# A graph kernel's first stage in groups of four blocks, with every fourth PSUM bank copied by VectorE

## What is computed

```python
e = concat(u, i)            # u = p_u * (diag_u[:, None] * x_u @ W_u) + x_u ; i likewise with W_i
h = adj @ (adj.T @ e)
out = (h - mu) * rsqrt(var + eps) * gamma + beta + x
x = layernorm(x + out)
```

## Time and profile before

| | us |
|---|---|
| median of 3 runs | 1492.0 |
| lowest and highest | 1490.86, 1493.19 |
| the profiled execution | 1491.23 |
| its span in the trace | 1489.4 |
| TensorE busy in the span | 1472.9 |
| VectorE busy | 612.3 |
| ScalarE busy | 257.8 |
| DMA queue of SyncE, share of 16 engines' span | 90.4% |

### The profile page before, as it was taken

The page is one execution under the profiler, slowest core; times in us unless marked ns, Lnnn a source line. Parts: engine busy times, 40 slices in busy tenths (PEclk is TensorE's granted clock), DMA queues, the critical chain, the costliest instruction groups (busy, mean ns, idle before and its releaser), DMA issues.

```text
span 1489.4 us, 17202 instructions
## 1 busy us (share of the span) xinstructions
PE 1472.9 (99%) x6462; PEld 683.0 (46%) x6462; DVE 612.3 (41%) x1281; ACT 257.8 (17%) x535; POOL 61.3 (4%) x66
## 2 busy tenths in 40 slices
PE   8999999999999999999999999999999999999997
PEld 6555555555555543334444344444444444444332
DVE  5755565655555568424332553324111021110432
ACT  3333334343434320000100000100000000000110
POOL 0000000000000002100000011010000000000010
PEclk9999999999999999999999999999999999999999
DMA  9999999999999998999988588876498869988997
GB/s 318 371 413 416 417 417 415 386 414 407 383 417 398 394 390 321 422 421 420 335 318 306 212 366 314 308 271 229 149 334 307 294 228 359 336 321 306 373 420 284
DMA packets 121537, 517.87 MB, mean 348 GB/s; under 512 B 20300, under 2 KB 20340, under 8 KB 71540
## 3 DMA queue, kind: packets, MB, share of 16 engines
q1 hardware_dynamic: 119568, 516.46, 90.4%
q10 hardware_dynamic: 1892, 0.35, 0.1%
HBM read 410.61 MB, written 106.17 MB: 347 GB/s over the span
## 4 chain that ended last, share of the span: by engine, by line
issue 99%; POOLq 0%; POOL 0%; DVE 0%
POOL power_out L539 0%; POOLq L537 0%; POOLq L539 0%; DVE rows L1024 0%; POOL ident L532 0%; POOLq L534 0%; POOL ident L534 0%; POOLq L1284 0%
## 5 line engine op out<-in xcount | busy, mean ns | idle before, releaser
L839 PE MATMUL ps_u<-blk,vectors 128*128 128x512 f32 (+1 forms) x1904 | 682.7, 594 | 1.3 <-DMA blk<-a_transposed 0.7
L839 PEld LDWEIGHTS ps_u<-blk,vectors 128*128 128x128 f32 (+1 forms) x1904 | 273.5, 170 | 369.8 <-issue 366.6
L578 ACT ACTIVATE blk<-ps_turn 128x512 f32<-128x512 f32 x400 | 202.2, 625 | 330.0 <-PE ps_turn L664 328.7
L1198 DVE TENSOR_TENSOR part<-part,ps_u 64x512 f32<-64x512 f32 (+1 forms) x40 | 27.4, 685 | 356.2 <-PE ps_u L839 355.8
L705 PE MATMUL ps_h<-blk,u_rows 128*64 128x512 f32 x720 | 164.4, 598 | 0.0
L940 DVE TENSOR_REDUCE row_part<-blk 128x4 f32<-128x2048 f32 x68 | 152.4, 2278 | 0.1
L924 DVE TENSOR_TENSOR part<-part,ps_h 128x512 f32<-128x512 f32 x80 | 55.0, 687 | 184.4 <-PE ps_h L705 184.4
L664 PE MATMUL ps_turn<-ident,blk 128*128 128x128 f32 x1072 | 126.0, 276 | 3.0 <-DMA blk<-in_adj 3.0
L664 PEld LDWEIGHTS ps_turn<-ident,blk 128*128 128x128 f32 x1072 | 117.8, 142 | 23.1 <-issue 19.5
L688 PE MATMUL ps_u<-blk,e 128*64 128x512 f32 x544 | 123.8, 594 | 0.0
L539 POOL TENSOR_TENSOR power_out<-power_in,minus_half 128x4 f32<-128x4 f32 x60 | 60.6, 1010 | 1424.4 <-DVEq L987 1424.4
(11 more groups left out here) (123 smaller groups left out, 625.2 us busy)
## 6 DMA issues: line engine op xcount, KB each, us to landing
blk<-a_transposed SPq DMA_DIRECT2D x276, 1024.0 KB, 6.6
a_transposed<-blk SPq DMA_DIRECT2D x100, 1024.0 KB, 14.2
blk<-in_adj SPq DMA_DIRECT2D x67, 1024.0 KB, 12.3
nat_far<-in_adj SPq DMA_DIRECT2D x32, 1024.0 KB, 12.8
early_blk<-a_transposed SPq DMA_DIRECT2D x12, 1024.0 KB, 8.0
nat_far<-a_transposed SPq DMA_DIRECT2D x2, 1024.0 KB, 11.3
rows<-in_x SPq DMA_DIRECT2D x10, 128.0 KB, 9.2
out<-rows SPq DMA_DIRECT2D x10, 128.0 KB, 3.5
```

The costliest lines, as they stand in the source:

```text
L578: nc.scalar.activation(blk[:, n % RING, t, :], ps_t[t][:, :], ACT.Copy)\
L839: mm = pe.matmul(acc, left, tiles[:, t, :], start=first, stop=last)
L1198: V.tensor_tensor(part[parts, cols], part[parts, cols], ps_both[r % 2][parts, :], ALU.add)\
```

## The change

The first column is put in another order. Rows of x are loaded ahead of their block, blocks 0 to 2 come in quarters, and the first e product stands in the middle of block 1's turn. The product x W is two matmuls with a block-diagonal W of 128 x 128 instead of four of 64 x 64, and has a place of its own in each of the two ps_h banks. The factors for users and for items have a semaphore each.

From block 10 on there are groups of four blocks (the last has two): four e products, then four h products, then four turns. `u_rows` becomes two tiles in turn (`u_columns`). From block 11 on ScalarE copies three banks of a block and VectorE the fourth (`evacuate_last_bank`), behind the four adds of the group.

Three smaller edits: two of the last h products move beside other blocks (`SOON_H`), the second last add moves ahead of a wait for a root (`soon`), and `add_y` waits for the last block of its own group of sums.

```diff
-    SOON_BEGUN, SOON_H = 3, 7
+    SOON_BEGUN, SOON_H = 3, {(1, 1): 7, (2, 2): 8}
...
+    IN_QUARTERS, GROUP = 3, 4
...
-                sp.wait_ge(at_evacuated, TB * (n + 1))
+                sp.wait_ge(at_evacuated, act_evacuated(n))
+                if n > NB:
+                    sp.wait_ge(last_bank_evacuated, n - NB)
...
-                if n == 0:
-                    for c in range(TB - 1):
-                        sp.dma_start(nat(0)[:, c, :], a_blocks[:, c, 0:BLK]).then_inc(quarter_loaded[c], 16)
-                    sp.dma_start(nat(0)[:, TB - 1, :], a_blocks[:, TB - 1, 0:BLK]).then_inc(nat_loaded[0], 16)
+                if n < NB:
+                    tiles = slice(n * TB, (n + 1) * TB)
+                    sp.dma_start(rows[:, tiles, :], x_rows[:, tiles, :]).then_inc(x_loaded[n], 16)
+                if n < IN_QUARTERS:
+                    for c in range(TB):
+                        sp.dma_start(nat(n)[:, c, :], a_blocks[:, n * TB + c, 0:BLK])\
+                            .then_inc(quarter_loaded[n][c] if c < TB - 1 else nat_loaded[n], 16)
                 else:
                     sp.dma_start(nat(n), a_blocks[:, i * TB:(i + 1) * TB, j * BLK:(j + 1) * BLK])\
                         .then_inc(nat_loaded[n % NAT], 16)
-                if n < NB:
-                    tiles = slice(n * TB, (n + 1) * TB)
-                    sp.dma_start(rows[:, tiles, :], x_rows[:, tiles, :]).then_inc(x_loaded[n], 16)
                 for k in range(n_behind(n - 1), n_behind(n)):
                     store(k)
...
-                for t in range(TB):
+                for t in range(TB if n <= NB else TB - 1):
                     act.wait_ge(turned, TB * n + t + 1)
                     nc.scalar.activation(blk[:, n % RING, t, :], ps_t[t][:, :], ACT.Copy)\
                         .then_inc(at_evacuated, 1)
...
-                if i > 0:
-                    pe.wait_ge(xw_used, i)
+                if i == 0:
+                    pe.wait_ge(w0_cleared, 1)
                 pe.wait_ge(w_i_loaded if i >= UB else consts_loaded, 32 if i >= UB else 16 * N_CONSTS)
-                for t in range(TB):
-                    xw_t = (xw_even if t % 2 == 0 else xw_odd[i % 2])[:, t // 2, :]
-                    mm = pe.matmul(xw_t, x_in_turned[i % 2][half(t), t // 2 * P:(t // 2 + 1) * P],
-                                   w0[half(t), int(i >= UB), :], start=True, stop=True)
+                for u in range(HT):
+                    mm = pe.matmul(xw_in[i % 2][:, u * P:(u + 1) * P], x_in_turned[i % 2][:, u * P:(u + 1) * P],
+                                   w0[:, int(i >= UB)].rearrange("p k f -> p (k f)"), start=True, stop=True)
                 mm.then_inc(xw_ready, 1)
...
+            def turn_quarters(n, between={}):
 
                 for c in range(TB):
                     if c < TB - 1:
-                        pe.wait_ge(quarter_loaded[c], 16)
+                        pe.wait_ge(quarter_loaded[n][c], 16)
                     else:
-                        pe.wait_ge(nat_loaded[0], 16)
+                        pe.wait_ge(nat_loaded[n], 16)
                     for t in range(TB):
-                        mm = pe.transpose(ps_t[t][:, c * P:(c + 1) * P], nat(0)[:, c, t * P:(t + 1) * P], ident[:, :])
+                        if c == 0 and n > 0:
+                            pe.wait_ge(at_evacuated, TB * (n - 1) + t + 1)
+                        mm = pe.transpose(ps_t[t][:, c * P:(c + 1) * P], nat(n)[:, c, t * P:(t + 1) * P], ident[:, :])
                         if c == TB - 1:
                             mm.then_inc(turned, 1)
+                    if c in between:
+                        between[c]()
...
             def h_part(n):
                 pe.wait_ge(u_ready, n // NB + 1)
-                pe.wait_ge(at_evacuated, TB * (n + 1))
+                pe.wait_ge(at_evacuated, act_evacuated(n))
+                if n > NB:
+                    pe.wait_ge(last_bank_evacuated, n - NB)
...
-            turn_first()
+            def first_e():
+                turn_diag()
+                times_w(0)
+
+            def first_u():
+                u_part(0)
+                times_w(1)
+
             turn_x_in(0)
-            turn_diag()
-            times_w(0)
-            for n in range(NB):
-                turn_block(n + 1)
+            turn_quarters(0, {1: first_e})
+            turn_x_in(1)
+            turn_quarters(1, {1: first_u})
+            for n in range(1, NB):
                 if n + 1 < NB:
                     turn_x_in(n + 1)
                 u_part(n)
                 if n + 1 < NB:
                     times_w(n + 1)
-            for p in range(COLUMN, BLOCKS // 2):
-                u_part(2 * p)
-                u_part(2 * p + 1)
-                if p % COLUMN == 0:
-                    u_turn_back(p // COLUMN - 1)
-                if p > COLUMN:
-                    turn_block(2 * p)
-                turn_block(2 * p + 1)
-                if p == BLOCKS // 2 - 1:
+                if n + 1 < IN_QUARTERS:
+                    turn_quarters(n + 1)
+                else:
+                    turn_block(n + 1)
+            def turn_group(four):
+                for n in four:
+                    if n > NB:
+                        turn_block(n)
+
+            for four in groups:
+                last = four[-1] == BLOCKS - 1
+                for n in four:
+                    u_part(n)
+                if last:
+                    turn_group(four)
                     u_turn_back(NB - 1)
-                h_part(2 * p - NB)
-                h_part(2 * p + 1 - NB)
+                for n in four:
+                    if n % NB == 0 and (n == NB or n != four[0]):
+                        u_turn_back(n // NB - 1)
+                for n in four:
+                    h_part(n - NB)
+                if not last:
+                    turn_group(four)
+                    if four[-1] % NB == NB - 1:
+                        u_turn_back(four[-1] // NB)
...
-                    if k != SOON_H:
+                    if k not in SOON_H.values():
                         last_h_part(k)
                 for b in row_0[e - 1] if 1 <= e <= NB - 2 else ():
-                    if blocks[b][1:3] == (1, 1):
-                        last_h_part(SOON_H)
+                    if blocks[b][1:3] in SOON_H:
+                        last_h_part(SOON_H[blocks[b][1:3]])
                     multiply_block(b)
...
-                diag_i = diag[:, tiles].rearrange("p (t k) -> p k t", k=2)
-                for k in range(2):
-                    V.tensor_tensor(by_pairs(ta)[:, k], (xw_even, xw_odd[i % 2])[k],
-                                    diag_i[:, k].unsqueeze(2).broadcast_to([P, HT, F]), ALU.mult)
+                V.tensor_tensor(ta[:, :, :], xw_in[i % 2].rearrange("p (t f) -> p t f", t=TB),
+                                diag[:, tiles].unsqueeze(2).broadcast_to([P, TB, F]), ALU.mult)
...
-                V.reduce_sum((u_rows if j < NB - 1 else u_last)[:, :, :], back_halves[j % 2], AX.X).then_inc(u_ready, 1)
+                V.reduce_sum(u_columns[j % 2][:, :, :], back_halves[j % 2], AX.X).then_inc(u_ready, 1)
...
             copy_x_in(0)
-            dve.wait_ge(par_loaded, 32)
-            V.tensor_tensor(par_prod[:, :], par[:, :, 0], par[:, :, 1], ALU.mult)
-            dve.drain()
-            dve.wait_ge(diag_turned, 1)
-            V.tensor_scalar(diag[:, 0:UT], diag_in[:, 0:UT], par_prod[:, 0:1], None, ALU.mult)
-            V.tensor_scalar(diag[:, UT:NT], diag_in[:, UT:NT], par_prod[:, 1:2], None, ALU.mult)
-            dve.drain()
+            dve.wait_ge(par_u_loaded, 16)
+            weigh_diag(0, slice(0, UT))
             make_e(0)
-            for c in range(TB - 1):
-                dve.wait_ge(quarter_loaded[c], 16)
             for n in range(NB):
                 if n + 1 < NB:
                     copy_x_in(n + 1)
+                for c in range(TB - 1 if n < IN_QUARTERS else 0):
+                    dve.wait_ge(quarter_loaded[n][c], 16)
                 sum_rows(n)
+                if n == 1:
+                    dve.wait_ge(par_i_loaded, 16)
+                    weigh_diag(1, slice(UT, NT))
                 if n + 1 < NB:
                     make_e(n + 1)
             copy_u(0)
-            for p in range(COLUMN, BLOCKS // 2):
-                sum_rows(2 * p)
-                sum_rows(2 * p + 1)
-                if p % COLUMN == 0:
-                    copy_u_rows(p // COLUMN - 1)
-                if p % COLUMN == COLUMN - 1:
-                    copy_u(p // COLUMN)
-                if p == BLOCKS // 2 - 1:
+            def evacuate_last_bank(n):
+                dve.wait_ge(turned, TB * (n + 1))
+                dve.wait_ge(at_stored[n % RING], 16 * (n // RING))
+                V.tensor_copy(blk[:, n % RING, TB - 1, :], ps_t[TB - 1][:, :]).then_inc(last_bank_evacuated, 1)
+
+            for four in groups:
+                last = four[-1] == BLOCKS - 1
+                for n in four:
+                    sum_rows(n)
```

(67 more changed lines are left out.)

13 lines of the change are left out of this document (11 added, 2 removed).

## The result

The changed kernel takes **1566.1 us**, the kernel before 1492.6 in the same runs: a ratio of 1.0487, 95% interval [1.0465, 1.0509]. It was forecast slower, by 8.8 us; it is slower by 73.6.

The account below looks back on a forecast made before the run. TensorE, busy 1472.9 of 1489.4 us, was taken as the bound. The terms summed to +8.8 on the profiled 1491.2, giving 1500.0, or 1500.8 us for the median; range 1488 to 1509.

Parts of the forecast that it names:

- Term d: Groups of four: loads 0.6 early, but 2.0 late at blocks 40, 60 and 80; +6.0 us, bounds 0 and 10.
- Term a: First stage: fewer changes between kinds of TensorE work, 0.32 a round saved 22 times; -7.0 us.
- Term b: First group, blocks 10 to 13: TensorE waits 0.9 and 3.5 on VectorE; +4.4 us, bounds 3.5 to 4.6.
- Term c: ScalarE's constant loads behind blocks 11 and 15 delay evictions, waits about 1.2 and 3.8; +5.0 us, from 0 to 5.3.
- Term e: Between two groups: VectorE's chain of copy, sums and add comes late in some groups; +4.8 us, bounds 2.5 and 13.
- Term f: Five groups: turning back u between the two products instead of beside turns adds two changes of kind; +1.6 us.
- Term g: First column: earlier first product and shorter rounds, less 1.3 for the lower clock; -3.6 us, bounds -5.5 and -1.5.
- Term h: The ends: a turn in the first layer's end no longer waits, -1.0; an add in the last sweep, -1.4 us.
- transfers have room: Rival: DMA queue not full, issues take 0.33, loads land in time; sum -2.3, 1489.7 us; chance 0.24.
- transfers are the bound: Rival: at 2.7 a transfer, a group's eight need 21.6, so every group waits 0.6; 1506 us; chance 0.10.
- VectorE is the bound: Rival: VectorE's chain between groups is 0.45 longer and 22 groups pay it; 1510 us; chance 0.10.
- a rival for quarters: First column: six more transfers at a fixed 2 us each, one after another, 12 us; chance no more than 0.01.

Follow-up runs that it names:

- e4: The changed kernel with one store later, so SyncE issues the loads of a group's third and fourth block in a row: 1510.9 us, ratio 1.014.
- e7: The changed kernel with third and fourth h product behind the turns, two loads in a row, ScalarE's constants behind a group's last block: 1487.2 us, ratio 0.9976.
- e9: e7 with u turned back beside turns and, in the first group, two of VectorE's sums behind its bank copies: 1483.4 us, ratio 0.9957.

## Why the prediction was wrong, step by step

The sign, and most steps, were right. Two steps failed, and they make 66.6 of the 68.4 us by which the spans differ more than the sum said.

- **Term d, mis-sized: 6.0 forecast, 48.5 measured.** The place was right: the fourth load, freed by the second turn, against 10.55 us. The queue's time was wrong: 9.95 forecast, 12.6 measured in the group shown. The 1.75 for latency came from quarters of a block, landing in 2.8; the whole block into the empty queue, with a store right behind it, took 6.1, not 0.4 + 2.6 + 1.75 = 4.75, and the store 3.9 more, not 2.6, which was read from a queue that never ran dry. I counted on 0.6 of spare in 19 of 22 groups, where an error of 2.6 turns every group around: the groups that I named, of blocks 40, 60 and 80, wait 4.80, 3.33 and 4.29, and the other 31.7 stand in sixteen groups that I had as early. The range 0 to 10 was built from the stores, not from this latency. No row of before shows such a burst. Its nearest one, a single load of a sweep into an empty queue with no other issued for 17 us, is close to my 4.75 and would not have warned me:

```profile
L507 SPq DMA_DIRECT2D blk<-a_transposed x1: 319/319/319, 1047.2 to 1047.2; - x1
...
DMA to landing us min/median/max: 4.8/4.8/4.8
```

  How much of the 1.3 between 4.8 and 6.1 comes from the store that is issued 0.5 behind, and how much from the load being of adj, no run separates.

- **The step that was missing: the clock, 24.1.** I charged 1.3 for the clock in the first column and nothing for the waits that I forecast in the groups, though the row I used shows the clock at 0.50 behind a wait of 3.0. By that row the forecast's own waits of 3.5 and 3.8 should have been priced at over a microsecond each: e4, which keeps these two as its only long waits (3.6 and 5.0), pays 3.8.
- **Term a** -7.0 forecast, -6.4 measured: 21.03 for a group without waits (e4, whose order is after's), two rounds of before 21.32.
- **Term b** +4.4, measured 0.78 + 3.61. Right to the row.
- **Term c** +5.0, measured 6.6: 0.90 and 5.74, forecast 1.2 and 3.8 (of these the forecast's own figures, 0.3 + 2.3 + 0.6 - 2.2, make 1.0, not 1.2). ScalarE's eight issues behind block 15 took 7.0 (101.44 to 108.46), where 5.1 was read from the earlier trace rows; the wait grew by the same 1.9. TensorE's rows, then ScalarE's:

```profile
101.67 1.91 PE L678 MATMUL ps_turn<-ident,nat_far 128*128 128x128 f32 x16
109.32 3.65 PE L678 MATMUL ps_turn<-ident,nat_far 128*128 128x128 f32 x16 [5.74 <-ACT blk L593]
...
101.44 0.47 ACTq L560 DMA_DIRECT2D turn<-in_L_gnn_W  x1
...
107.64 0.82 ACTq L560 DMA_DIRECT2D w_copy<-in_L_gnn_weight  x1
108.58 1.58 ACT L593 ACTIVATE blk<-ps_turn 128x512 f32<-128x512 f32 x3 [6.36 <-issue]
```

- **Term e** +4.8, measured 0: VectorE catches up while TensorE waits for loads. In e4, without these, 2.0 remain, in four groups; in e7 and e9 none; there the add behind the sums is wanted only behind the next turns.
- **Term f** +1.6, measured about +1.5: turning back between e and h products costs 0.74 (e7: 21.76 against 21.02 for a group), beside turns 0.44 (before: 11.10 against 10.66 for a round), and after has it between products in the five groups named. Right.
- **Term g** -3.6, measured -1.6. The first product came at 12.56 (forecast 12.2), but two quarters of block 1's turns, 0.87, are now behind it, which I had booked as gained. A round fell from 4.58 to 4.47, by 0.11, not 0.22. What these leave, 1.2, is about the 1.3 charged for the clock. This term isn't firm: in the other runs' traces block 10 starts between 56.3 and 59.4.
- **Term h and the last sweep** -2.4, measured -1.1: TensorE waits 0.75 for VectorE a little later in the layer's end (637.63), and 0.80 are left of the 1.4 in the earlier trace rows.

Of the rivals, "transfers have room" and "transfers are the bound" both fall: in after the queue idles and is late all the same, in e7 it is full and in time. "VectorE is the bound" finds no wait of TensorE on VectorE in after behind the first group. The Trainium skill, SBUF — State Buffer, section The DMA setup-cost knee, gives each transfer some 2 us of its own, which got 0.01 as a rival for quarters; what I should have asked is what it says of a *whole* block into an empty queue. The fit in that section of the Trainium skill comes to an estimated 4.4 us for 1 MB. The single load of a sweep took 4.8, not far from it, but the 6.1 measured in the group is above both and above my 4.75, so neither would have saved the forecast.

## What to carry to other kernels

A rate that is read from a full queue doesn't hold for one that runs empty: ask whether the change makes releases come in bursts, and if no row shows a burst into an empty queue, put that into the range. Where a forecast rests on a spare of 0.6 us against a sum of five read times, its range is the number of groups times the error of that sum. And a wait of several microseconds on TensorE is to be booked with its clock: here 55 us of waits brought 24 more.

## What the runs showed that was not expected

- Six loads of 1 MB in after's stage went into an empty queue, each with a store issued 0.4 to 0.8 behind. They landed after 5.2 to 7.6 us, and the store behind 2.5 to 3.9 later; the same queue full takes 5.2 for a load and a store.
- Behind long waits TensorE worked at half speed, 48.2 us in eleven groups, and so came later to free the next buffers. The Trainium skill, TensorE: Matmul & The Clock Gate, section Loop structure matters more than you think, warns of DMA waits between products for that reason; the traces agree. From block 38 on, groups that wait about 3 us or more mostly alternate with ones that wait 0.5 to 2.3; that a slow group gives the queue time would explain it, and is not shown.
- Beside its length in the rows, each wait on a load costs about 0.2: seven groups of after at the full clock, with one wait and no column's end, take 21.24 beside it, where 21.03 is a group that doesn't wait.
